# A ViT block on one core: score bias as 64-row products with high and low rows side by side, filler products from a constant, value factors and row of scales made apart

## What is computed

```
h = patches @ W.T + b + pos_emb                      # 512 x 256, K = 768
k, q, v = split(layernorm(h) @ W_kqv + b_kqv)        # 16 heads of 16
attn = softmax(q @ k.T / sqrt(16) + slopes * tril(j - i), masked for j > i)
h = h + (attn @ v) @ W_proj + b_proj                 # attention inside an image
z = layernorm(h)
hid = bitlinear(z, w_fc) + gate * (z @ v.T @ fast_b.T @ u.T)   # hidden 1024, rank 16
h = h + bitlinear(relu(hid) ** 2, w_proj)
# bitlinear(x, w): scale = mean(|w|) per output row,
#                  x @ (clip(round(w / scale), -1, 1) * scale).T
```

## Time and profile before

| | |
|---|---|
| runs | 71.11, 71.55, 71.77 us |
| the profiled execution | 70.84 us, its span 69.0 us |
| busy, of the span | PE 90%, PEld 80%, DVE 66%, ACT 56%, POOL 37% |
| chain, by line | embedding 13%, output layer 11%, hidden layer 8%, scores 5%, filler products 5% |

### The profile page before, as it was taken

How to read it: one execution, slowest core, us unless ns; L and a number is a source line. 1 busy time by engine, 2 the same in 40 slices (tenths; PEclk the granted TensorE clock), 3 DMA queues, 4 the chain that set the end, 5 groups by cost and what they waited for, 6 DMA issues and landing times.

```text
span 69.0 us, 2144 instructions
## 1 busy us (share of the span) xinstructions
PE 61.9 (90%) x886; PEld 55.6 (80%) x886; DVE 45.6 (66%) x99; ACT 38.4 (56%) x76; POOL 25.9 (37%) x41
## 2 busy tenths in 40 slices
PE   3999999999989999999999967999976999999900
PEld 2787888889979999897988836989936899999900
DVE  1000029567999877997999783426596999969670
ACT  5200001824395969947779996737949338964000
POOL 6400408597779389999915000000000000000610
PEclk9999999999999999999999999999999999999997
DMA  0899999999810000000000000000000000000053
GB/s 0 269 310 312 321 385 410 419 362 369 311 64 0 9 0 0 0 9 0 9 0 0 9 5 5 0 0 9 0 0 0 0 0 0 0 0 0 9 176 128
DMA packets 3497, 6.74 MB, mean 98 GB/s; under 512 B 400, under 2 KB 1312, under 8 KB 3488
## 3 DMA queue, kind: packets, MB, share of 16 engines
q1 hardware_dynamic: 3488, 6.60, 26.5%
HBM read 6.08 MB, written 0.52 MB: 96 GB/s over the span
## 4 chain that ended last, share of the span: by engine, by line
PE 69%; DVE 12%; ACT 12%; issue 3%
PE psum L304 13%; PE psum L489 11%; PE psum L460 8%; PE psum L370 5%; PE psum L499 5%; PE psum L324 4%; PE psum L344 4%; PE psum L427 3%; PE psum L399 2%; DVE z L779 2%; PE psum L388 2%; PE psum L469 2%; ACT L696 2%; ACT fc_t L614 2%; PE psum L437 2%
## 5 line engine op out<-in xcount | busy, mean ns | idle before, releaser
L1043 POOL TENSOR_TENSOR tail_sb<-tail_sb,h 128x256 f32<-128x256 f32 x2 | 1.4, 732 | 26.3 <-DVE tail_sb L878 26.3
L719 ACT ACTIVATE head_sb<-psum,fc_scale 128x256 f32<-128x256 f32 x16 | 6.7, 470 | 4.6 <-PE psum L469 3.7
L593 ACT ACTIVATE std<-mv,eps_sb 128x1 f32<-128x1 f32 x8 | 2.2, 288 | 12.5 <-DVE mv L773 12.5
L489 PE MATMUL psum<-mlp_t,sq_hi 128*128 128x256 f32 x32 | 7.9, 285 | 1.1 <-DVE sq_lo L797 1.0
L489 PE MATMUL psum<-mlp_t,sq_lo 128*128 128x256 f32 x32 | 7.7, 281 | 0.0
L769 DVE TENSOR_TENSOR h<-psum,pos_sb 128x256 f32<-128x256 f32 x4 | 1.6, 412 | 8.9 <-PE psum L304 8.9
L489 PEld LDWEIGHTS psum<-mlp_t,sq_hi 128*128 128x128 f32 x32 | 6.0, 189 | 1.5 <-issue 1.5
L460 PE MATMUL psum<-zt_hi,fc_t 128*128 128x256 f32 x32 | 6.7, 281 | 0.0
L304 PE MATMUL psum<-head_sb 128*128 128x256 f32 x24 | 6.7, 445 | 0.0
L460 PE MATMUL psum<-zt_lo,fc_t 128*128 128x256 f32 x32 | 6.6, 278 | 0.0
L304 PEld LDWEIGHTS psum<-head_sb 128*128 128x128 f32 x24 | 5.5, 235 | 1.0
(11 more groups left out here) (111 smaller groups left out, 164.7 us busy)
## 6 DMA issues: line engine op xcount, KB each, us to landing
head_sb<-head SPq DMA_DIRECT2D x6, 256.0 KB, 4.2
fc_sb<-w_fc SPq DMA_DIRECT2D x2, 512.0 KB, 7.0
mlp_sb<-w_mlp SPq DMA_DIRECT2D x2, 512.0 KB, 8.9
tail_sb<-tail SPq DMA_DIRECT2D x2, 384.0 KB, 6.1
out<-tail_sb SPq DMA_DIRECT2D x4, 128.0 KB, 1.7
pos_sb<-pos SPq DMA_DIRECT2D x1, 256.0 KB, 4.6
kqv_sb<-w_k SPq DMA_DIRECT2D x1, 256.0 KB, 6.5
kqv_sb<-w_q SPq DMA_DIRECT2D x1, 256.0 KB, 6.7
```

Of the source, the lines that this page charges most:

```text
L489: mm = pe.matmul(mlp_ps[f * BH + b], part[:, n % RING, a, b * P:(b + 1) * P], mlp_t[:, 2 * j + a, :], start=j == 0 and a == 0 and i == 0 a ...
L719: nc.scalar.activation(relu[:, n % PART_RING, a, :], FCB[n][:, a * HT:(a + 1) * HT], ACT.Relu, scale=fc_scale[:, 0, m:m + 1]).then_inc(rel ...
```

## The change

Four edits, of which two are tied together:

- **Filler products.** `warm`, its clearing on VectorE and TensorE's wait for it are gone. The 14 products now read `const-bfloat16-1.0`, a column of ones that the program's preamble sets anyway, repeated over 128 and 256 columns.
- **Bias.** Each bank of scores has its own 64 rows of the array, as the scores do. Row p of `bias_t` holds the slopes of the bank p // 64; its 64 rows are twice 32, rows 0 to 31 with the rounded values and rows 32 to 63 with the rest. `select_r` has a one where p mod 32 is the query, so that one product of 64 rows adds high and low part. Two products in place of four for each half; the tables have half the columns (8 heads x 16 keys), and the rest is subtracted by two operations of 32 rows.
- **Value factors.** `fold_v` stays where both were, with its own place in the bank, its own copy (32 columns, no longer waiting for the scales of the output layer) and its own semaphores.
- **Row of scales.** `spread_scale` is called between the first turn of the second layernorm and `turn_mlp(1)`. Its copy (256 columns) stands on ScalarE after the second `mlp_signs`. The second turn waits for it, as it takes the same bank.

```diff
-        warm = sb("warm", [P, HT], BF16)
+        ones = nc.const_aps.tensor(1.0, [P, HT], BF16)
...
             def score_bias(f):
-                pe.wait_ge(alibi_step, 4)
-                pe.wait_ge(identr_done, 1)
+                pe.wait_ge(alibi_step, 5)
+                pe.wait_ge(select_done, 1)
                 for r in range(2):
-                    for i, part in enumerate((alibi_hi, alibi_lo)):
-                        bias = part[:, r * HPG:(r + 1) * HPG, :].rearrange("p (o h) s -> p o (h s)", o=1)
-                        pe.matmul(s_ps[f][:, r, :], ident_r[:, :], bias.broadcast_to([P, BH, HPG * S]),
-                                  start=i == 0, stop=False, skip_group_check=True)
+                    rows = slice(r * 64, (r + 1) * 64)
+                    bias = bias_t[rows, :, :].rearrange("p (o h) s -> p o (h s)", o=1)
+                    pe.matmul(s_ps[f][:, r, :], select_r[rows, :, :].rearrange("p h s -> p (h s)"),
+                              bias.broadcast_to([64, BH, HPG * S]), start=True, stop=False, skip_group_check=True)
...
-            def fold_v_spread_scale():
+            def fold_v():
                 pe.wait_ge(v0_in, 16)
+                for k in range(KE):
+                    mm = pe.matmul(vf_ps[:, k * RANK:(k + 1) * RANK], v_sb[:, k * P:(k + 1) * P], v_sb[:, E:E + RANK],
+                                   start=True, stop=True)
+                mm.then_inc(vf_done, 1)
+
+            def spread_scale():
                 pe.wait_ge(mlp_scaled, 1)
...
                 for m in range(KE):
...
-                mm.then_inc(side_done, 1)
+                mm.then_inc(row_done, 1)
...
-            pe.wait_ge(warm_set, 1)
             for _ in range(WARM_PRODUCTS):
-                pe.matmul(bank[7][:, 0:HT], warm[:, 0:P], warm[:, :], start=True, stop=True)
+                pe.matmul(bank[7][:, 0:HT], ones[:, 0:P], ones, start=True, stop=True)
...
-            fold_v_spread_scale()
+            fold_v()
             project(0)
-            pe.wait_ge(side_copied, 1)
+            pe.wait_ge(vf_copied, 1)
             turn_mlp(0)
...
             turn(0, z, z2t_ps[0], z2_ready, z2t_turned)
+            spread_scale()
             pe.wait_ge(duo_ready, 6)
             turn_mlp(1)
...
+            pe.wait_ge(row_copied, 1)
             turn(1, z, z2t_ps[1], z2_ready, z2t_turned)
...
             fc_signs(0)
-            copy_out(side_sb[:, :], side_ps, side_done, 1, side_copied)
+            copy_out(vf_sb[:, :, :], vf_ps.rearrange("p (k r) -> p k r", r=RANK), vf_done, 1, vf_copied)
             fc_signs(1)
...
             mlp_signs(1)
+            copy_out(scale_row[:, :], row_ps, row_done, 1, row_copied)
...
-            dve.memset(warm[:, :], 0.0).then_inc(warm_set, 1)
...
-                pool.tensor_tensor(alibi_lo[:, :, :], alibi[:, :, :], alibi_hi[:, :, :].bitcast(F32),
-                                   ALU.subtract).then_inc(alibi_step, 1)
+                for r in range(2):
+                    low = slice(r * 64 + 32, (r + 1) * 64)
+                    pool.tensor_tensor(bias_t[low, :, :], alibi[low, :, :], bias_t[low, :, :].bitcast(F32),
+                                       ALU.subtract).then_inc(alibi_step, 1)
...
+    c[:, C_SEL:C_SEL + S] = p[:, None] % (2 * S) == np.arange(S)[None, :]
```

More of the change, by code:

```diff
@@ L49 @@
 C_SLOPE = C_IMG + 2
-C_GATE = C_SLOPE + H
+C_SEL = C_SLOPE + HPG
+C_GATE = C_SEL + S
 C_QB = C_GATE + 1
@@ L79, in build_program @@
         v_sb = sb("v_sb", [RANK, E + RANK])
-        side_sb = sb("side_sb", [P, KE * RANK + E])
-        vf_sb = side_sb[:, 0:KE * RANK].rearrange("p (k r) -> p k r", r=RANK)
-        scale_row = side_sb[:, KE * RANK:KE * RANK + E]
+        vf_sb = sb("vf_sb", [P, KE, RANK])
+        scale_row = sb("scale_row", [P, E])
         ident = const_sb[:, C_ID:C_ID + P]
@@ L89, in build_program @@
         img_mask = const_sb[:, C_IMG:C_IMG + 2]
-        slope = const_sb[:, C_SLOPE:C_SLOPE + H]
+        slope = const_sb[:, C_SLOPE:C_SLOPE + HPG]
+        select = const_sb[:, C_SEL:C_SEL + S]
         gate = const_sb[:, C_GATE:C_GATE + 1]
@@ L101, in build_program @@
         abs_junk = sb("abs_junk", [P, HID], BF16)
[L102 to L105, removed]
+        select_r = sb("select_r", [P, HPG, S], F32R)
+        alibi = sb("alibi", [P, HPG, S])
+        bias_t = sb("bias_t", [P, HPG, S], F32R)
         kqv_hi = sb("kqv_hi", [P, 3, KE, E], F32R)
@@ L160, in build_program @@
         s_ps = [psum[:, 1:3, 0:HT], psum[:, 4:6, 0:HT]]
-        side_ps = bank[3][:, 0:KE * RANK + E]
+        vf_ps = bank[3][:, 0:KE * RANK]
+        row_ps = bank[3][:, E:2 * E]
         y_ps = [psum[:, 0:4, 0:HT], psum[:, 4:8, 0:HT]]
@@ L182, in build_program @@
         out_done = sem("out_done")
-        warm_set = sem("warm_set")
         eps_set = sem("eps_set")
@@ L187, in build_program @@
         posb_done = sem("posb_done")
-        identr_done = sem("identr_done")
+        select_done = sem("select_done")
         round_set = sem("round_set")
@@ L202, in build_program @@
         mlpt_ready = sem("mlpt_ready")
-        side_done, side_copied = sem("side_done"), sem("side_copied")
+        vf_done, vf_copied = sem("vf_done"), sem("vf_copied")
+        row_done, row_copied = sem("row_done"), sem("row_copied")
         u_step = sem("u_step")
@@ L401, in project @@
                     mm.then_inc(o_done, 1)
-            def fold_v_spread_scale():
+            def fold_v():
                 pe.wait_ge(v0_in, 16)
+                for k in range(KE):
[3 more added lines that the diff above has]
+            def spread_scale():
                 pe.wait_ge(mlp_scaled, 1)
-                for k in range(KE):
-                    pe.matmul(side_ps[:, k * RANK:(k + 1) * RANK], v_sb[:, k * P:(k + 1) * P], v_sb[:, E:E + RANK],
-                              start=True, stop=True)
                 for m in range(KE):
-                    c = KE * RANK + m * P
-                    mm = pe.matmul(side_ps[:, c:c + P], mlp_scale[:, 0, m:m + 1].broadcast_to([P, P]), ident,
+                    mm = pe.matmul(row_ps[:, m * P:(m + 1) * P], mlp_scale[:, 0, m:m + 1].broadcast_to([P, P]), ident,
                                    start=True, stop=True)
-                mm.then_inc(side_done, 1)
+                mm.then_inc(row_done, 1)
             def turn_u():
@@ L876, in scale_result @@
                     dve.wait_ge(mlp_step, 2 * STEPS)
-                dve.wait_ge(side_copied, 1)
-                dve.tensor_tensor(out_sb[:, b, :], mlp_ps[b], scale_row, ALU.mult).then_inc(out_scaled, 1)
+                dve.wait_ge(row_copied, 1)
+                dve.tensor_tensor(out_sb[:, b, :], mlp_ps[b], scale_row[:, :], ALU.mult).then_inc(out_scaled, 1)
             def add_result(b):
@@ L967, in bias_tables @@
                 pool.wait_ge(const_in, 16)
-                rel_, neg_ = (t.rearrange("p (o s) -> p o s", o=1).broadcast_to([P, H, S]) for t in (rel, neg))
-                pool.tensor_scalar(ident_r[:, :], ident, 1.0, 1.0, ALU.mult, ALU.mult).then_inc(identr_done, 1)
+                rel_, neg_, select_ = (t.rearrange("p (o s) -> p o s", o=1).broadcast_to([P, HPG, S])
+                                       for t in (rel, neg, select))
+                pool.tensor_scalar(select_r[:, :, :], select_, 1.0, 1.0, ALU.mult, ALU.mult).then_inc(select_done, 1)
                 pool.tensor_tensor(alibi[:, :, :], rel_, slope.rearrange("p (h o) -> p h o", o=1).broadcast_to(
-                    [P, H, S]), ALU.mult).then_inc(alibi_step, 1)
+                    [P, HPG, S]), ALU.mult).then_inc(alibi_step, 1)
                 pool.wait_ge(alibi_step, 1)
@@ L1015, in value_factors @@
             def value_factors():
-                pool.wait_ge(side_copied, 1)
+                pool.wait_ge(vf_copied, 1)
                 hi, lo = v_fold[:, :, 0, 0, :], v_fold[:, :, 0, 1, :]
-                pool.tensor_scalar(hi, vf_sb, 1.0, 1.0, ALU.mult, ALU.mult).then_inc(fold_step, 1)
+                pool.tensor_scalar(hi, vf_sb[:, :, :], 1.0, 1.0, ALU.mult, ALU.mult).then_inc(fold_step, 1)
                 pool.wait_ge(fold_step, 1)
-                pool.tensor_tensor(lo, vf_sb, hi.bitcast(F32), ALU.subtract).then_inc(fold_step, 1)
+                pool.tensor_tensor(lo, vf_sb[:, :, :], hi.bitcast(F32), ALU.subtract).then_inc(fold_step, 1)
                 pool.wait_ge(fold_step, 2)
```

6 lines of the change are left out of this document (3 added, 3 removed).

## The result

The changed kernel is slower: 72.13 us as the median of four runs (71.86 to 72.76), against 71.33 (70.79 to 71.77) for the kernel before in four; the ratio is 1.0187 with a 95% interval of 1.013 to 1.0244. Forecast were 71.25 us and a gain of 0.30. The profiled execution took 72.19 us with a span of 70.40, against 70.84 and 69.04.

What follows compares the result with a forecast made beforehand. TensorE, with 69% of the chain, was taken to bound the kernel. Start and bias gains, limited to 0.30 us at the second scores and carried to the end, took the median from 71.55 to 71.25 us; range 70.5 to 71.75.

Steps and rivals of the forecast that it cites:

- carried to the end: Whole kernel: 0.30 us earlier at 28 and again at 42 us reaches the end, 70.84 becoming 70.5 in the profiled execution.
- the slower one (stretched fillers): Start: fillers reading one repeated column take 4.7 us instead of 3.0; 0.73 later, 72.3 us; chance 0.08.
- Start: 0.19 forecast: Warm-up: TensorE starts 0.25 us earlier without the clearing and its wait, so the embedding ends 0.19 earlier.
- halved a gain: Embedding: work before the clock's rise runs at half pace, so its end moves (0.12 + 0.25) / 2 = 0.19 us.
- Bias: 0.20 forecast: First bias table: two 64-row products replace four of 128 rows, gaining 0.20 us between 0.15 and 0.27.
- two products side by side: First bias table: both products run at once, 0.09 + 0 + 0.21 = 0.30 us to the first score, a gain of 0.27.
- the last step: First bias table: from the last bias product to the first score, taken as 0.21 us.
- At the second scores: Near 28 us: scores start 0.30 us earlier, at 27.78; GpSimd's key spread gains only 0.19, giving back 0.09 of bias gain.
- 35 to 42 us: 0.30 forecast: Value factors to the stretch's end at 42.14: VectorE's variance, and so the end, moves only by the scores' 0.30 us.
- the 0.6 forecast: ScalarE by 37.7 us: no wait of 0.47 and a smaller copy put it some 0.6 us ahead.
- rival 1: Clock or transfers favour the start more: 0.85 us gained, 70.7; VectorE's unexplained pause at 39 could add 0.3; chance 0.20.
- Row of scales: covered, as forecast: Before `turn_mlp(1)`: the row's 0.55 us ends at 42.11, inside TensorE's wait until 42.14; its ScalarE copy costs at most 0.1.

Runs made afterwards that it cites:

- pe_pad4: The changed kernel with four 16-column TensorE products added behind `fold_v()`; ratio 0.9925 to the kernel before, median 70.70 us.
- only_warm: The kernel before with the filler edit alone (`ones` for `warm`, no clearing, no wait); ratio 0.9991 to the kernel before.
- only_bias: The kernel before with the bias edit alone; ratio 0.9945 to the kernel before.
- dve_pad1: The changed kernel with one clearing of a spare tile added at VectorE's start; ratio 1.013 to the kernel before.
- no_row_wait: The changed kernel without TensorE's wait for `row_copied` ahead of the second turn; ratio 0.9941 to the kernel before.
- pe_pad3_b: The changed kernel with three 16-column TensorE products added behind `fold_v()`, measured again; ratio 0.9928 to the kernel before.
- late_pad4: The changed kernel with four 16-column TensorE products added after the last output product; ratio 0.9936 to the kernel before.
- fill11_b: The kernel before with 11 filler products in place of 14, measured again; ratio 1.0032 to the kernel before.
- fill12: The kernel before with 12 filler products in place of 14; one run, 72.23 us.

## Why the prediction was wrong

**The step that failed is the sum's last: "carried to the end".** The 0.30 was carried to the end of the work (measured 0.28), and I took the output behind it as fixed. It isn't: the tail grew by 3.78 - 2.14 = 1.64 us, and 1.64 - 0.28 = 1.36 is the difference of the spans. In all 18 kernels the tail is 3.2 to 3.8 where the last fetch starts between the start and the end of the output (six kernels), and 2.1 to 2.3 where it doesn't (twelve). With the fetch moved out of the output by pe_pad4 the change gains 71.01 - 70.70 = 0.31 us by the medians, near the forecast, but that is luck: the terms below are off and make up for one another. None of my rivals was this one; the slower one (stretched fillers) isn't seen, since 14 fillers still take 3.15 us. The seven packets of kind "instruction" stood on the page of the kernel before, and the transfer view has the last 1.2 us ahead of the first output packet; the change takes instructions out of TensorE's stream. That the fetch would move was to be read; to which side, not.

**Start: 0.19 forecast, none measured.** The filler did start 0.28 earlier, but VectorE's first sum came 0.09 later. The clock's level rose sooner than in the kernel before, and then the chunks were what the products waited for, 1.9 us in all. The forecast halved a gain on the assumption that the transfers aren't waited for; with a sooner rise they are. only_warm, whose ratio holds 1, has a gain of 0.06 at the first sum (9.85) without a sooner rise: its fillers start at 0.77 too, but the embedding waits 0.54 for the first chunk and starts at 3.98. One execution can't settle a term of this size: over the fourteen kernels with 14 fillers the first sum comes between 9.26 and 10.22.

**Bias: 0.20 forecast, 0.15 measured.** From the last value product to the first score it was 21.88 - 21.20 = 0.68 us, and is 21.80 - 21.27 = 0.53. The first bias product comes 0.21 behind the value product where like products stand 0.12 apart, so the added change of form costs 0.09. The second starts with the first (3 to 4 ns apart in all eleven kernels with this edit), which is the prediction's case of two products side by side, with a gain of 0.27. The term that was mis-sized is the last step: from there to the first score it is 0.32, not 0.21, and so 0.11 of the gain is lost. That each of these products is recorded with 0.38 instead of 0.28 is seen as well; why is open. only_bias agrees, with 0.52 for 0.68. The Trainium skill (TensorEngine Tiling, Key Properties) has the engine drain at a change of tiling mode; the steps of 0.21 and 0.32 agree with a cost, 0.09 and 0.20 above a step of 0.12. At the second scores it was 0.06 earlier instead of 0.30. There both copies hardly moved: ScalarE's ends at 27.93 for 28.03, and GpSimd's spread at 27.87 for 27.92. The lost start took 0.19 of it from both. That GpSimd keeps the scores from the bias gain, as I had it, is not seen; TensorE's weight loads are recorded as waiting for ScalarE there.

**35 to 42 us: 0.30 forecast, 0.28 measured, by another way.** ScalarE was ahead, by more than the 0.6 forecast (the second `fc_t` starts at 35.67, where it was 36.60), and TensorE waited 0.41 for `yt`. But then VectorE lost a pause. Before, this row stands in its timeline:

```profile
39.16 0.42 DVE L769 TENSOR_TENSOR h<-psum,h 128x256 f32<-128x256 f32 x1 [0.33 <-issue]
```

In the change the same sum starts at 38.68 without a wait. The pause, 0.30 to 0.33 long, is there in all nine kernels in which VectorE has 128 recorded instructions, dve_pad1 among them, and in none of the nine with 127. So removing the clearing of `warm` removed it, which rival 1 had named as unexplained. It is worth the whole gain of this stretch: from the second scores to the second turn of the output layer's weights TensorE needs 42.14 - 28.08 = 14.06 us in the kernel before, 41.86 - 28.02 = 13.84 in the change, and 42.22 - 28.15 = 14.07 in dve_pad1, which is the change with the pause. So the 0.28 is 0.06 that came over from the scores, where 0.30 was forecast, and 0.22 from a pause that the sum didn't count; that it is close to 0.30 is luck. VectorE's variance ends 0.50 sooner, and TensorE gains 0.28 of it, held by ScalarE's last copy of `y_duo`.

**Row of scales: covered, as forecast.** It starts at 41.26 and its neighbours at 41.86, with a wait for `y_duo` recorded before them; `low_t` isn't late by its new neighbour on ScalarE, it is 0.28 sooner. The wait for `row_copied` costs nothing where it stands, and 1.6 us of tail by being an instruction (3.8 against 2.1 in no_row_wait).

## What to carry to other kernels

Before a change of a few tenths of a microsecond is costed, look in the transfer view for the packets of instructions, and see which transfers that are waited for lie within a microsecond or two of them; the output at the end has nothing to hide it. When a small edit costs more than its work can, compare the stretch behind the last instruction first, and then pad the engine whose stream was cut: four products of 16 columns, or one wait less, turned 1.0187 into 0.9925 and 0.9941 here, and are with pe_pad3_b and late_pad4 the fastest versions found. The place belongs to one program, so it is to be checked again after every further edit.

## What the runs showed of the hardware

One 16 KB instruction fetch amid the output cost 1.1 to 1.6 us of tail (3.2 to 3.8 for 2.1); its own packet took 0.90 us in the change and 1.36 to 1.75 in the other five. The Trainium skill (Runtime: NRT & Kernel Launch, Instruction fetch mechanics) says that instructions are refilled in blocks of 16 KiB by a DMA queue of the engine's own, at a cost that is "mostly hidden". The trace agrees with the size and with a queue that holds nothing else; the cost didn't show in the tail of twelve of these kernels and did in six.

Two products of 64 rows in different rows of the array and different banks started 3 to 4 ns apart.

TensorE also stood still for 0.49 to 0.89 us at "issue" in the first scores of some kernels (pe_pad4, fill11_b, fill12), and VectorE for 0.3 at 39 us. TensorE's pauses hold no fetch: they start at 22.95, 23.55 and 23.73 and end by 24.44, the fetch before them ended at 22.05, 23.10 and 22.90, and no packet of any kind begins between 22.7 and 24.5. Open stay what in TensorE's stream sets the last fetch's time, and why two engines' pauses come and go with one instruction.
